# A graph-and-attention layer with experts: x tiles filed three to four steps ahead, attention matrices formed behind the last filing steps, the completeness flag used as the keys' factor, and the start of the second aggregation rearranged

## The reference, cut to what matters

```python
edge_index_t = stack([src, dst], axis=1)            # 106250 edges, sorted by dst, 6250 nodes
xn = layernorm(x)                                   # x: 6250 x 256
def graph_conv(x, edges, W0, b0, W1, b1):           # every edge counts in both directions
    deg = maximum(segment_sum(ones, dst), 1)
    agg = segment_sum(x[src], dst) / deg
    return x @ W0 + b0 + agg @ W1 + b1
gnn = graph_conv(relu(graph_conv(xn, ...)), ...)    # widths 256 -> 512 -> 256
q, k, v = heads(xn @ Wq.T + bq), heads(xn @ Wk.T + bk), heads(xn @ Wv.T + bv)   # 8 heads of 32
mix = (q @ (k^T v / N)) @ Wfc.T + bfc               # linear attention: only small matrices of x
x = x + gnn + mix
t = layernorm(x)                                    # then 8 experts, the best 2 for each row
x = x + sum_over_top2(gate * (relu(t @ W1[e] + b1[e]) @ W2[e] + b2[e]))
```

## Time and profile before

| what | value |
|---|---|
| median of 3 runs | 2245.94 us (2245.6 to 2248.06) |
| profiled execution, its own time | 2241.64 us |
| span of the profiled execution | 2240.1 us |
| PE busy | 2075.8 us, 93% |
| DVE busy | 1551.8 us, 69% |
| ACT busy | 1198.9 us, 54% |
| POOL busy | 369.5 us, 16% |
| mean granted clock of PE | 0.973 |
| chain that ended last | PE 68%, issue 13%, DVE 8%, DVE's queue 4% |

### The profile page before, as it was taken

The page is one execution under the profiler, slowest core; times in us unless marked ns, Lnnn a source line. Parts: engine busy times, 40 slices in busy tenths (PEclk is TensorE's granted clock), DMA queues, the critical chain, the costliest instruction groups (busy, mean ns, idle before and its releaser), DMA issues.

```text
span 2240.1 us, 52353 instructions
## 1 busy us (share of the span) xinstructions
PE 2075.8 (93%) x15356; PEld 1310.5 (59%) x15357; DVE 1551.8 (69%) x4887; ACT 1198.9 (54%) x2466; POOL 369.5 (16%) x438
## 2 busy tenths in 40 slices
PE   3887888999999999999999988999999995999997
PEld 2676675555565555555454544444444443899996
DVE  6898987999999999999645544455555444455554
ACT  3677663555555555555656543444444443566664
POOL 2000000000000000000111111111111222466665
PEclk9999998999999999999999999999999997999998
DMA  3333227222222222222534336555555554565552
GB/s 94 90 89 96 81 96 210 116 116 113 111 114 116 116 116 114 110 111 116 179 132 166 111 115 227 194 194 200 199 201 198 192 194 162 138 97 92 90 92 43
DMA packets 158735, 299.12 MB, mean 134 GB/s; under 512 B 31774, under 2 KB 107855, under 8 KB 156419
## 3 DMA queue, kind: packets, MB, share of 16 engines
q1 hardware_dynamic: 131075, 243.66, 31.3%
q0 software_dynamic: 25856, 47.15, 9.3%
q10 hardware_dynamic: 1664, 6.35, 0.8%
HBM read 148.32 MB, written 144.19 MB: 131 GB/s over the span
## 4 chain that ended last, share of the span: by engine, by line
PE 68%; issue 13%; DVE 8%; DVEq 4%; DMA 2%; POOLq 2%; POOL 1%; ACT 1%; ACTq 0%; SPq 0%
PE bank L2272 44%; PE bank L2263 6%; PE bank L2513 6%; PE bank L2498 6%; DVEq L1166 2%; POOLq L843 1%; DVE big L1123 1%; DVE big L1136 1%; PE bank L2480 1%; DVEq L1132 1%; DVE big L1118 1%; PE bank L2280 1%; DVE big L1134 1%; DMA big<-rows_dram 1%; PE bank L2141 1%
## 5 line engine op out<-in xcount | busy, mean ns | idle before, releaser
L2272 PE MATMUL bank<-RW,big 128*128 128x512 f16 x4753 | 1149.1, 380 | 0.0
L2272 PEld LDWEIGHTS bank<-RW,big 128*128 128x128 f16 x4753 | 431.6, 98 | 385.0 <-issue 3.6
L1920 ACT ACTIVATE big<-bank 128x512 f16<-128x512 f32 (+1 forms) x640 | 364.2, 573 | 316.5 <-PE bank L2263 316.4
L1294 DVE TENSOR_TENSOR big<-iotaB,keys 128x512 f16<-128x512 f16 x1300 | 451.9, 417 | 7.9 <-issue 6.8
L2263 PEld LDWEIGHTS bank<-big 128*128 128x128 f16 x2560 | 190.9, 98 | 106.2 <-issue 1.4
L2263 PE MATMUL bank<-big 128*128 128x128 f16 x2560 | 247.5, 219 | 0.4 <-issue 0.4
L977 POOL DMA_INDIRECT out_dram<-big x112 | 179.9, 1606 | 110.1 <-ACT big L2066 74.7
L910 POOL DMA_DIRECT2D big<-in_L_ffn_W_dram x8 | 6.2, 778 | 1052.5 <-DVE R L1353 1051.7
L2057 ACT ACTIVATE big<-bank,b1A,iscA 128x256 f32<-128x256 f32 x224 | 114.2, 560 | 98.2 <-PE bank L2498 93.6
L2513 PE MATMUL bank<-RW,big 128*128 (+1 forms) x1344 | 157.7, 274 | 0.4 <-DVE big L1717 0.3
L2498 PE MATMUL bank<-big,RW 128*128 128x256 f16 x1344 | 156.3, 273 | 0.4 <-ACT big L2046 0.4
(11 more groups left out here) (421 smaller groups left out, 2925.4 us busy)
## 6 DMA issues: line engine op xcount, KB each, us to landing
big<-a_dram SPq DMA_DIRECT2D x48, 800.0 KB, 6.0
big<-a_dram SPq DMA_DIRECT2D x48, 768.0 KB, 4.3
a_dram<-big SPq DMA_DIRECT2D x49, 640.0 KB, 2.9
a_dram<-big SPq DMA_DIRECT2D x49, 512.0 KB, 2.6
a_dram<-big SPq DMA_DIRECT2D x49, 416.0 KB, 2.4
big<-rows_dram SPq DMA_DIRECT2D x56, 265.0 KB
big<-in_x_dram SPq DMA_DIRECT2D x96, 128.0 KB, 2.1
own_dram<-big SPq DMA_DIRECT2D x48, 256.0 KB, 2.5
```

The lines of the kernel that those rows point to most:

```text
L1294: last = v.tensor_tensor(out[q].rearrange("p b (m k) -> p b m k", k=2), inturn(iotaB[:, :], QB, P // 2), twice(kd[:, q * QB:(q + 1) * QB, ...
L1920: a.activation(Ab[q][:, 0:n], banks[BB(q)][:, 0:n], ACT.Copy).then_inc(s_ab, 1)
L2272: last = mm(bank[:, :], blk(q, c), R2[:, u * 2 * D:(u + 1) * 2 * D], start=(i == 0), stop=(i == T - 1))
```

## The change

It has five parts.

1. **x ahead.** The x work of step t (`normal1`, `deviation1`, `gram`, `own1`, `place1`, `low1`, the loads and stores) is now that of tile t+3 up to t = 20, both t+3 and t+4 at t = 20, and t+4 from there on. Three steps of it stand ahead of the loop. `ones` and `epsc` are set first on POOL, `deviation1(0)` and `(1)` run before the window loads, `inverse(0)` and `(1)` right after the counts.
2. **Attention matrices** up to the head blocks are formed in four pieces `mixed1(0..3)` behind the filing of the last four steps, on PE and ACT, in other banks.
3. **The count** of `cover` is made by PE with a ones matrix in five products of at most 512 columns into one bank, then summed by DVE. TT and TU are no longer multiplied by `fit`; the keys are.
4. **The rest of the first seam** is spread: the product with `WfT` stands between the two sets of flip products, the rest behind the second set.
5. **Second seam.** `tile0` waits for each of the last seven tiles of R2 when it comes to it, and not for all before it begins; the gate bias product stands behind it. The last expert's steps are spread: on DVE `iterate2(1)` stands ahead of `scales(7)`, and `iterate2(2)` ahead of its `lows`; on ACT `norms(7)` and `highs(7, 0)` stand behind `iterate(1, 1)` and `highs(7, 1)` behind `iterate(1, 2)`. On POOL the waits and the store of expert 7 (`kept`) stand behind the overflow test, still ahead of `weights(0)`. SP's load of `b2b` moves from tile 1 to the end of the aggregation.

```diff
+FILL = 3
+CATCH = 20
+def x_steps(t):
+    if t < CATCH:
+        return [t + FILL]
+    if t == CATCH:
+        return [t + FILL, t + FILL + 1]
+    return [t + FILL + 1]
...
 # SP
+            load_x(0)
             for name, dst in (("L0_mix_Wq", Wq), ...  8 weights
+            load_x(1)
...
+            load_x(2)
+            for j in range(FILL - 1):
+                store_xT(j)
             for t in range(T):
...
-                if t + 3 < T:
-                    sp.wait_ge(s_xn, t + 1)
...
+                for j in x_steps(t):
+                    load_x(j)
+                    if j <= T:
+                        store_xT(j - 1)
+                    if j >= 4:
+                        store_own(j - 4)
...
             rows_x(1)
-            sp.wait_ge(s_wst, 16 * EXPERTS)
-            sp.dma_start(b2b.rearrange("p e n -> p (e n)"), ...).then_inc(s_b2, 16)
             load_a(3, 1, 2)
             rows_x(2)
             with sp.Fori(1, T // 2 - 1) as k: ...
+            sp.wait_ge(s_wst, 16 * EXPERTS)
+            sp.dma_start(b2b.rearrange("p e n -> p (e n)"), ...).then_inc(s_b2, 16)
 # POOL
+            drawn(0, True)
+            kept(0, True)
+            with pool.Fori(1, EXPERTS - 1) as e:
+                drawn(e)
+                kept(e)
+            drawn(EXPERTS - 1)
             pool.wait_ge(s_yl, 1 + T)
             pool.wait_ge(s_zc, 3 + T)
             with pool.If(lacking > 0):
                 overflow(1)
+            kept(EXPERTS - 1)
 # DVE
             v.tensor_copy(cntS[:, 0:T], cntF).then_inc(s_start, 1)
+            inverse(0)
+            inverse(1)
...
-            inverse(0)
+            inverse(2)
             words1(0)
             keys1(0)
+            inverse(3)
...
-                if t + 1 < T:
-                    inverse(t + 1)
+                for j in x_steps(t + 1):
+                    if j < T:
+                        inverse(j)
...
-            v.tensor_reduce(small[:, 56:57], cover, AX.X, ALU.add).then_inc(s_flag, 1)
-            dve.wait_ge(s_fp, 2)
...
-            v.tensor_scalar(TT[:, 0:T * TC], TT[:, 0:T * TC], fit[:, 0:1], None, ALU.mult)
-            v.tensor_scalar(TU[:, 0:T * TC], TU[:, 0:T * TC], fit[:, 0:1], None, ALU.mult).then_inc(s_flag, 1)
+            v.tensor_scalar(cover, TT[:, 0:T * TC], 0.5, None, ALU.is_ge).then_inc(s_flag, 1)
+            dve.wait_ge(s_fp, 2)
+            v.tensor_reduce(small[:, 56:57], banks[4][:, :], AX.X, ALU.add)
...
             iterate2(0, None, None)
+            iterate2(1, (0, 0), None)
             scales(EXPERTS - 1)
+            iterate2(2, (1, 1), (0, 0))
             for j in range(2):
                 lows(EXPERTS - 1, j)
-            iterate2(1, (0, 0), None)
-            iterate2(2, (1, 1), (0, 0))
 # ACT, filing loop
+            for j in range(FILL):
+                if j:
+                    normal1(j)
+                step1(j)                      # own1(j - 3), deviation1(j + 2), place1(j), low1(j)
             base1(0)
             for t in range(T):
+                for n, j in enumerate(x_steps(t)):
+                    if j < T:
+                        normal1(j)
+                    if n == 0:
+                        if t + 1 < T:
+                            base1(t + 1)
+                        if t:
+                            table1(t - 1)
+                    step1(j)
+                    if j >= T:
+                        mixed1(j - T)
...
             table1(T - 1)
 # ACT, second aggregation
                 iterate(L, 0, None, banks[5])
-                if L == 1:
-                    norms(EXPERTS - 1)
-                    for j in range(2):
-                        highs(EXPERTS - 1, j)
...
                     iterate(1, 1, (0, 0, None), banks[7])
+                    norms(EXPERTS - 1)
+                    highs(EXPERTS - 1, 0)
                     iterate(1, 2, (1, 1, None), banks[5])
+                    highs(EXPERTS - 1, 1)
 # PE, filing loop
+            for j in range(FILL):
+                step1(j)                      # gram(j), own1(j - 2)
             before1(0, 0)
             for t in range(T):
                 if t + 1 < T:
                     before1(t + 1, (t + 1) % 2)
-                gram(t)
-                if t >= 2:
-                    own1(t - 2)
+                for j in x_steps(t):
+                    step1(j)
                 file1(t, t % 2)
+                if t >= T - 4:
+                    mixed1(t + 4 - T)         # 2: L2198 to L2204, 3: L2209 to L2211
 # PE, first seam: flips of TT, product with WfT, flips of TU, L2225 to L2230, count, L2233
+            for c in range(0, T * TC, 4 * P):
+                n = min(4 * P, T * TC - c)
+                last = mm(banks[4][:, 0:n], ones16, cover[:, c:c + n], start=(c == 0), stop=(c + 4 * P >= T * TC))
 # PE, tile0
-                    if i == 0:
-                        pe.wait_ge(s_yl, 1 + T)
                     u = 0 if i == T - 1 else T - 1 if i == 0 else i
+                    if i == 1 or u >= T - W:
+                        pe.wait_ge(s_yl, 2 + max(u, T - W - 1))
```

More of the change, by code:

```diff
@@ L903, in _, with drawn @@
                 pool.wait_ge(s_st[i], 16 * T + 16)
-            def expert(e, first):
+            def drawn(e, first=False):
                 if first:
@@ L918, in expert, with kept @@
                 nc.gpsimd.partition_all_reduce(nr3, sq3, P, RADD).then_inc(s_wr, 1)
+            def kept(e, first=False):
                 wait(s_wh, 2 * e + 2)
@@ L1020, in inturn, with inverse @@
                 return ap.rearrange("p (a m k) -> p a m k", a=1, k=2).to_broadcast([P, n, m, 2])
+            def inverse(t):
+                i = t % 2
+                dve.wait_ge(s_std, t + 1)
+                if t >= 2:
+                    dve.wait_ge(s_xn, t - 1)
+                v.reciprocal(rstd[:, i:i + 1], sums[:, i, 3:4])
+                dve.drain()
+                v.tensor_tensor(offs[:, i:i + 1], sums[:, i, 1:2], rstd[:, i:i + 1], ALU.mult).then_inc(s_stat, 1)
+            v.memset(xs[:, D:D + 1], 1.0)
             dve.wait_ge(s_edges, 48)
@@ L1829, in _, with step1, mixed1 @@
-            deviation1(1)
+            def step1(j):
+                if 0 <= j - 3 <= T:
+                    own1(j - 3)
+                if j + 2 < T:
+                    deviation1(j + 2)
+                if j < T:
+                    place1(j)
+                    low1(j)
+            def mixed1(i):
+                if i == 0:
+                    for n in range(2):
+                        a.activation(PTs[:, n, :], zeros32[:, 0:D], ACT.Copy)
+                    act.wait_ge(s_pm, 4)
+                    a.activation(Gs[:, 0, :], banks[6][:, 0:D + 1], ACT.Copy)
+                    a.activation(Gs[:, 1, P:D + 1], banks[6][:, D + 1:2 * D + 2 - P], ACT.Copy).then_inc(s_vm, 1)
+                elif i == 1:
+                    act.wait_ge(s_gt, 1)
+                    a.activation(Gs[:, 1, 0:P], banks[4][:, 0:P], ACT.Copy).then_inc(s_gc, 1)
+                elif i == 2:
+                    act.wait_ge(s_pm, 5)
+                    a.activation(B1s, k2(banks[4][:, :]), ACT.Copy)
+                    a.activation(rows[0:1, SV, :], banks[6][0:1, 0:D], ACT.Copy)
+                    a.activation(rows[0:1, SK, :], banks[6][0:1, D:2 * D], ACT.Copy).then_inc(s_vm, 1)
+                elif i == 3:
+                    act.wait_ge(s_pm, 6)
+                    for h in range(HEADS):
+                        vt, g, w = h // 4, h % 4, D // HEADS
+                        last = a.activation(PTs[g * w:(g + 1) * w, vt, h * w:(h + 1) * w],
+                                            banks[5][g * w:(g + 1) * w, vt * D + h * w:vt * D + (h + 1) * w],
+                                            ACT.Copy, scale=1.0 / N)
+                    last.then_inc(s_vm, 1)
@@ L2184, in _ @@
                 if i == 0:
-                    mm(banks[6][:, 0:P], zeros16[:, :], zeros16[:, :], start=False, stop=True).then_inc(s_pm, 1)
-                    own1(T - 1)
-            own1(T)
-            pe.wait_ge(s_vm, 4)
-            pe.wait_ge(s_xe, T + 1)
-            nc.tensor.transpose(banks[7][:, 2 * P:3 * P], Gs[:, 0, P:D], ident[:, :]).then_inc(s_gt, 1)
-            pe.wait_ge(s_mrg, T // RB + 2)
-            for gt in (1, 0):
-                if gt == 0:
-                    pe.wait_ge(s_gc, 1)
+                    for dt in range(2):
+                        for et in range(2):
+                            last = mm(banks[6][:, dt * D:(dt + 1) * D], PTs[:, et, dt * P:(dt + 1) * P], WfT[:, et, :],
+                                      start=(et == 0), stop=(et == 1))
@@ L2202, in _ @@
[L2202 to L2211 removed]
+                mm(banks[6][0:1, 0:D], bqc[:, dt:dt + 1], Rs[:, dt, :], start=(dt == 0), stop=False)
```

265 lines of the change are left out of this document (112 added, 153 removed).

## The result

The changed kernel takes 2268.47 us in the median of 4 runs (2266.62 to 2270.95), the kernel before 2245.77 (2244.52 to 2248.06): a ratio of 1.0104, 95% interval 1.009 to 1.0118. It is 22.7 us slower; 14.6 were forecast. The four runs lie in two pairs, 2266.6 twice, at a mean granted clock of 0.971, and 2270.3 and 2271.0, at 0.966 and 0.967; the profile is of the second pair.

The account below looks back on a forecast made before the run. DVE's own list bounds filing, PE both aggregations, and a POOL DMA chain decides tile 3. Filing +4.2, first seam -1.5, second seam +11.9 give +14.6 on profiled 2241.64: 2256.2, median 2260.5 us; range 2249 to 2271.

Parts of the forecast that it names:

- first seam: From the last ranks' end to the first histogram, 42.2 us before: forecast -1.5 us (-5 to +2).
- Second seam: Stretch of 63 us around PE's last output product and tiles 0 to 3: forecast +11.9 us (+7 to +18.6).
- Filing: Stretch of 293 us up to the last ranks, taken as bound by DVE's own list: forecast +4.2 us (1 to 8).
- the start: First ranks held because own1(0), ahead of before1(0) on PE, waits for all 16 weight loads: +3.2 us (1 to 5).
- The 0.7 around the window start: Inverses and lane operations ahead of the window start, less what DVE's wait for ACT's deviation hides: +0.7 us.
- The catch-up: Extra x step at t = 20 in filing; second gram on PE waits for ACT's first low1: +1.2 us (0 to 3).
- R: End of the last ranks, from which the forecast dated decode and the histogram; 327.26 us in the kernel before.
- The restart: PE reaches the first histogram early, waits and starts again at the half clock: gives back 2.3 us.
- In both aggregations PE is full and the change leaves the work per tile alone.: Claim that PE bounds both aggregations and their time per tile stays unchanged; no cost was forecast there.
- The price of the two loads: weights(0) and weights(1) on POOL, 1 MB each, ahead of the first scatter: 12.2 us, against 8.8 by the skill's rule.
- the slow loads: Rival: drain and scatter at tile 0 as slow as before, sum +21.3 us, 2267 us; chance 0.15.

Follow-up runs that it names:

- the run with everything: Changed kernel plus both start waits off, windows early, second catch-up, tables scaled on ScalarE, GpSimd's loads and first scatter ahead of expert 7's store: 2231.29 us, 0.9931 of the kernel before.

## Why it came out so, by the steps of the prediction

- **Filing, +4.2 forecast, +9.4 measured.** Of its parts the start was furthest off. The 0.7 around the window start did not come: DVE still waited there for ACT's deviation, 7.1 for the 8.1 of before, and its first one-hots stood at 33.51 (before 33.54). `own1(0)` was named, but sized at the full clock and with a landing at 37: it started at 38.60 and took 3.78, so the stall was 7.0 and not 3.2. A second wait lay hidden under it, ACT's `deviation1(4)` ahead of `base1(0)`; the run with own1 late showed it by taking the first away. The prediction costed only what stands ahead of before1 on PE, not what stands ahead of base1 on ACT. And of SP's list it counted the weight loads, not the windows of group 1, now behind an x load that waits for `normal1`: +2.7 at step 3. The catch-up, +1.2 forecast, cost 0.6, and the four steps without an inverse gave 1.2 back.
- **First seam, -1.5 forecast, +2.1 measured at the count product.** Behind the last ranks, forecast and measured: decode 9.8 and 13.0, the histogram 38.4 and 41.3. So 3.2 of the 3.6 us lie ahead of decode. The chain of the matrices was priced from rows at the full clock, and here the granted clock was 0.50 around the end of filing and again in the second half of the fourth piece. In the two profiles of the same code in which the clock held, decode came at R + 9.4 and the seam gained 1.8 and 1.7 against the kernel before, close to the forecast. The work between decode and the histogram was right within 0.3 (28.6 forecast, 28.3 measured). The restart was taken at 2.3 and cost 3.0: PE begins earlier, is fed piecemeal, waits again for the digits, and the full clock came 16 us behind the first product instead of 6.
- **"In both aggregations PE is full and the change leaves the work per tile alone."** This step failed, and 5.5 us went there. I had read the flag as a factor for nothing per tile, since it replaces a factor of 1.0; the row for the new form did not exist, and I did not bound it. Even 0.06 us twice was too much, because DVE's period was within 0.03 us of PE's. The run with the constant factor gave the time back.
- **Second seam, +11.9 forecast, +8.9 measured.** Mechanism and links right. Behind the last output product, forecast and measured: tile 0's copy 16.3 and 16.3, its transposes 21.5 and 21.2, the store 47.4 and 44.3, weights(1) 56.3 and 52.7, end of the drain 61.2 and 58.3, scatter landed 66.6 and 63.2, tile 2's transposes 67.5 and 64.2. The 3 us lie ahead of the store: tile 2's copy came at 38.8 and not 40.8, the lows closer behind it. From the store on each link is within 0.7 us of the forecast. The drain lasted 5.45 for the 4.9 taken. That it waits for the landing, which I had left open, agrees with the run with the loads first, where it lasted as long as the store took to land. The price of the two loads was right within 1 us: 12.5 by the prediction's own dates (1365.4 to 1377.9; the 12.2 that it sets against 8.8 is 0.3 short), and 13.3 measured from the first issue to the end of the drain. By the fit of the Trainium skill ("DMA: Bandwidth & Descriptors", Anatomy of one DMA), 4.4 a load, an estimate of the two is 8.8. These two took 7.4 and 5.4 to land, so the rows of before were the better price.
- **What offset what.** In the profiles 28.6 us were lost for the 14.6 forecast. The second seam was forecast 3.0 too high; the first was 3.6 too low, filing 5.2, the aggregation 5.5, and 2.7 lie in the hidden stage and behind tile 3, where nothing was forecast. So the errors hardly offset each other. The medians differ by 22.7 only, since the profiled execution of before lay 4.1 below its median and that of after 1.8 above. The measured 2268.47 lies in the stated range, but above the 2253 to 2264 that had the most chance, and next to the 2267 of the slow loads, which did not happen: the second seam cost 8.9 and not 18.6. That the time falls in the range is in part luck; what was right is the direction and the second seam's mechanism.
- **Left open.** The hidden stage is 1.0 us longer in the changed kernel and 0.8 to 1.9 in those derived from it (259.5 to 260.7 from tile 48's count product to the last output product, 258.7 before), with nothing in its waits to name. No run settles it, nor the 1.7 us behind tile 3, nor why the clock fell at the end of filing in some executions.

## What to carry to other kernels

Before calling an engine the bound of a stretch, compare the periods of all engines in it, not their busy shares: DVE at 92% busy was 0.03 us a tile slower than a full PE, and had no slack for 0.12. For a wait that a reorder adds, follow every engine's own list up to the common consumer; taking one wait away often only uncovers the next (own1, deviation, windows, x). In a queue that drains before each wait, such as GpSimd's here, put what someone waits for (the scatter) ahead of what nobody waits for yet (the store), which took 14.8 of the change's 22.7 us of loss away by itself; with the other repairs the kernel is 15.5 faster than before. And one profile is one execution: before a seam is explained, look at its granted clock in the profiles of other kernels with the same code there.

## What the runs showed of the hardware

- Going between an all-reduce and an ordinary operation cost GpSimd 5.7 us one way and 7.0 the other, hidden or not depending on where the next ordinary operation stood. In the run with everything, with a 1 MB load under way, the way back took 8.5.
- Two of GpSimd's drains lasted until the transfer issued ahead of them had landed: behind `weights(1)` the drain ended at 1392.97 and the load landed at 1392.81, and with the loads first it was 1385.78 for a store that landed at 1385.69.
- A 128x2496 scaling on GpSimd (6.6 us) beside a VectorE operation of 0.27 us made that last 5.78.
- VectorE's 128x104 scaling took 215 ns with a constant and 274 ns with a per-partition factor.
- PE's granted clock was 0.61 from 366 to 385 us, with PE busy for 12.9 of these 19 us and waiting twice (2.29 and 3.41), and 1.00 in the 6 us behind.
- The same code at the end of filing ran at a granted clock of 0.50 in one execution and of 1.00 in another (329.5 to 336 us), and decode came 3.6 us later behind the last ranks in the first.
